# Down weights in four parts, eight rows turned in the first attention, the whole fold in the experts, and a reordered second attention

## What is computed

```python
h = tok(x, W, b)                                   # 256 x 512, patches of 128 samples
h = h + attn0(layernorm(h), Wq, Wk, Wv, Wp)        # 16 heads, ternary weights, int8-like rounding
h = h + moe(layernorm(h), router, gate, up, down)  # 16 experts of width 192, top 2 of them
h = h + attn1(layernorm(h), Wq, Wk, Wv, Wo)        # 16 heads, 4 key heads, causal
h = h + ffn1(layernorm(h), SU_ug, SU_dp, Wscale_ug, Wscale_dp, W_up, W_gate, W_down)

def ffn1(x, ...):                 # n = 512, inner width 2048
    x = fwht(x * SU_ug) / 64      # Walsh-Hadamard transform of width 512
    x_up   = x @ W_up.T   * (Wscale_ug[:2048] * 64)
    x_gate = x @ W_gate.T * (Wscale_ug[2048:] * 64)
    x = silu(x_gate) * x_up
    x = fwht(x * SU_dp) / 64      # transform of width 2048
    return x @ W_down.T * (Wscale_dp * 64)
```

## Time and profile before

| | |
|---|---|
| three runs | 284.29, 284.68, 285.15 us; median 284.68 us |
| the profiled execution | 285.33 us device time, span 283.5 us |
| mean granted clock of PE in it | 0.984 of full speed |
| busy in the span | PE 267.1 us (94%), DVE 228.1 (80%), ACT 148.7 (52%), POOL 6.4 (2%) |
| 40.43 MB moved, mean | 143 GB/s |

### The profile page before, as it was taken

How to read it: one execution, slowest core, us unless ns; L and a number is a source line. 1 busy time by engine, 2 the same in 40 slices (tenths; PEclk the granted TensorE clock), 3 DMA queues, 4 the chain that set the end, 5 groups by cost and what they waited for, 6 DMA issues and landing times. The chain is left out here.

```text
span 283.5 us, 3968 instructions
## 1 busy us (share of the span) xinstructions
PE 267.1 (94%) x1492; PEld 220.5 (78%) x1492; DVE 228.1 (80%) x410; ACT 148.7 (52%) x233; POOL 6.4 (2%) x19
## 2 busy tenths in 40 slices
PE   8789489999999999999999999999999999999993
PEld 3445355858899998989999887775589999999872
DVE  1979998797999978797798876798898895778783
ACT  2898760145563565555565514444457562663530
POOL 0200000000000000000000000000000000000000
PEclk9999959999999999999999999999999999999998
DMA  6960499944244807173530087193000000000003
GB/s 233 424 243 1 116 408 391 410 194 132 91 163 173 333 17 318 45 290 115 218 114 0 0 296 298 28 407 161 0 0 2 0 2 0 0 2 0 0 5 74
DMA packets 6565, 40.43 MB, mean 143 GB/s; under 512 B 1169, under 2 KB 1425, under 8 KB 5266
## 3 DMA queue, kind: packets, MB, share of 16 engines
q1 hardware_dynamic: 6546, 40.18, 36.9%
HBM read 39.13 MB, written 0.52 MB: 140 GB/s over the span
## 5 line engine op out<-in xcount | busy, mean ns | idle before, releaser
L1089 PE MATMUL bank<-s_xf_hi,s_f_hi 128*128 128x256 f32 x128 | 31.4, 284 | 0.0
L1089 PE MATMUL bank<-s_xf_hi,s_f_lo 128*128 128x256 f32 x128 | 31.1, 281 | 0.0
L530 ACT ACTIVATE s_silu<-bank 128x192 f32<-128x192 f32 x32 | 10.5, 331 | 36.6 <-PE bank L868 32.6
L868 PE MATMUL bank<-s_w_hi,s_xt_hi 128*128 128x384 f32 (+1 forms) x128 | 29.2, 350 | 0.0
L868 PE MATMUL bank<-s_w_lo,s_xt_hi 128*128 128x384 f32 (+1 forms) x128 | 27.9, 339 | 0.3 <-DVE s_w_lo L1416 0.3
L868 PE MATMUL bank<-s_w_hi,s_xt_lo 128*128 128x384 f32 (+1 forms) x128 | 27.8, 338 | 0.3 <-DVE s_xt_lo L1179 0.3
L1089 PEld LDWEIGHTS bank<-s_xf_hi,s_f_hi 128*128 128x128 f32 x128 | 24.1, 188 | 1.0 <-issue 0.5
L1089 PEld LDWEIGHTS bank<-s_xf_hi,s_f_lo 128*128 128x128 f32 x128 | 24.1, 188 | 0.4
L1642 DVE TENSOR_TENSOR s_f_lo<-s_ffn_raw,s_f_hi 128x1024 fp32r<-128x1024 f32 x16 | 19.6, 1224 | 5.3 <-ACT s_f_hi L610 5.2
L868 PEld LDWEIGHTS bank<-s_w_lo,s_xt_hi 128*128 128x128 f32 x128 | 22.7, 188 | 0.7 <-DVE s_w_lo L1416 0.7
L868 PEld LDWEIGHTS bank<-s_w_hi,s_xt_lo 128*128 128x128 f32 x128 | 22.8, 188 | 0.5 <-DVE s_xt_lo L1179 0.5
(11 more groups left out here) (241 smaller groups left out, 570.7 us busy)
## 6 DMA issues: line engine op xcount, KB each, us to landing
s_moe_raw<-moe_gu SPq DMA_DIRECT2D x16, 768.0 KB, 6.6
s_ffn_raw<-ffn_w SPq DMA_DIRECT2D x4, 2048.0 KB, 10.0
s_moe_raw<-moe_dn SPq DMA_DIRECT2D x8, 768.0 KB, 4.4
s_big_raw<-att_w SPq DMA_DIRECT2D x4, 1024.0 KB, 8.2
s_big_raw<-down_w SPq DMA_DIRECT2D x1, 4096.0 KB, 18.4
s_l_raw<-l_w SPq DMA_DIRECT2D x1, 2560.0 KB, 25.0
out<-s_h SPq DMA_DIRECT2D x4, 128.0 KB, 2.3
s_tok_w<-tok_w SPq DMA_DIRECT2D x1, 256.0 KB, 2.7
```

The costliest lines, as they stand in the source:

```text
L530: act.activation(B["silu"][i % 2][:], unit_bank(i)[:, 0:F], ACT.Silu).then_inc(silu_done, 1)
L868: ins = pe.matmul(unit_bank(i)[:, 0:n], xt(k, t)[part % 2], w[:, k, 0:n], start=(first and k == 0), stop=(last and k == KC - 1))
L1089: pe.matmul(tb(j, n)[:, 0:TOK], M[w][j][:, k, n * P:(n + 1) * P], M["xf_hi"][:, k, :], start=(w == "w_hi" and k == 0), stop=False)
```

## The change

It has four parts, all in the order of the written-out lists.

1. `down_w` comes in four transfers of 1 MB (rows 0 to 3, 4 to 7, 8 to 11, 12 to 15), each with its own semaphore. The first three are issued between the transfers of `k_swapped` and `v_swapped`, after `side_done` of 6; the fourth stands where the whole one stood.
2. Eight rows are turned in the first attention instead of four: three behind the product of line 822, ahead of the ternary copy; one for each tile in the place of seven filling products; three where three stood before. The one behind the transposes of the experts' input goes. The copies back on ACT move with them: three ahead of the casts of `tern_p`.
3. All 18 operations of the fold stand in the experts (`fold_step(0)` to `fold_step(17)`), three per pair, one of them ahead of `hidden(4 * p)`. `last_fold` goes.
4. In the second attention five turns are spread differently and four go: the turn inside `values(1)`, the turn behind `values(0)` (the identity product with `h` takes its place, so PE adds the residual of tile 0 and ACT copies the sum to `h`), one of three ahead of `values(1)` and the one ahead of the feed-forward. `exp(2)` stands ahead of `kv_out(1)`. DVE's `centred` for tile 0 stands ahead of the two `low_half`.

```diff
@@ names and tables
-        ld_l1, ld_down = sem("ld_l1"), sem("ld_down")
+        ld_l1 = sem("ld_l1")
+        ld_down = [sem(f"ld_down{g}") for g in range(4)]
-        TURNS = (0, 4, 8, 12, 10, 14, 11, 15, 1, 5, 9, 13, 2, 6, 3, 7)
-        TURN_BANK = (7, 3, 7, 3, 5, 1, 5, 1, 5, 1, 2, 5, 0, 4, 0, 4)
-        TURNS_FIRST = 4
+        TURNS = (0, 1, 4, 5, 8, 9, 12, 13, 10, 14, 11, 15, 2, 6, 3, 7)
+        TURN_BANK = (3, 7, 5, 3, 7, 3, 7, 3, 5, 1, 5, 1, 5, 0, 4, 0)
+        TURNS_FIRST = 8
@@ SP
+                if n == 0:
+                    sp.wait_ge(side_done, 6)
+                    for g in range(3):
+                        down_part(g)
...
             sp.wait_ge(side_done, 8)
-            sp.dma_start(big_raw[:], down_w).then_inc(ld_down, 16)
+            down_part(3)
@@ ACT
             exp(0, A["sc"][:, 2], A["sc"][:, 3])
+            for i in range(3):
+                turned_back(i)
             for k in range(KC):
                 act.wait_ge(tern_done, k + 1)
...
             xt_high(0)
+            turned_back(3)
             xt_high(1)
+            turned_back(4)
...
-            for i in range(3):
+            for i in range(5, TURNS_FIRST):
                 turned_back(i)
             xt_high(2)
-            turned_back(3)
...
+            exp(2, L["sc"][:, 2, 0, 0:2], L["sc"][:, 3, 0, 0:2])
             kv_out(1)
-            exp(2, L["sc"][:, 2, 0, 0:2], L["sc"][:, 3, 0, 0:2])
...
             f_high(1)
+            act.wait_ge(proj_done, 3)
+            act.copy(h[:, 0, :], tb(0, 3)[:]).then_inc(h_kept, 1)
             exp(3, L["sc"][:, 2, 1, 0:4], L["sc"][:, 3, 1, 0:4])
@@ PE
-                if i == 0:
-                    pe.wait_ge(ld_down, 16)
+                pe.wait_ge(ld_down[TURNS[i] // 4], 16)
...
+            pe.wait_ge(v16_ready, TILES)
+            turn(0)
+            turn(1)
+            pe.wait_ge(half_ready, 4)
+            turn(2)
             pe.wait_ge(q16_ready, TILES)
...
             for t in range(TILES):
+                pe.wait_ge(turned, t + 1)
                 for c in range(2):
...
                 transposes(t, A["xn"], t)
-                keep_warm(bank[3], FILL)
+                turn(3 + t)
...
                 for s in range(keys):
-                    if s == 2:
-                        turn(11)
                     pe.wait_ge(val_ready, 2 * t + s + 1)
...
             values(0)
-            turn(7)
+            pe.matmul(tb(0, 3)[:], ident, h[:, 0, :], start=True, stop=False)
...
-            for i in (8, 9, 10):
-                turn(i)
-            pe.wait_ge(turned, 11)
+            turn(11)
+            turn(12)
             values(1)
...
-            turn(15)
@@ DVE
             for p in range(2, PAIRS - 1):
                 main_low(2 * p + 1)
                 rest_low(2 * p + 1)
+                fold_step(3 * p - 4)
                 hidden(4 * p)
...
-                fold_piece(p - 1)
+                fold_step(3 * p - 3)
+                fold_step(3 * p - 2)
...
-            fold_piece(PAIRS - 2)
+            fold_step(17)
...
-            dve.wait_ge(proj_done, 3)
-            o.mark(dve.tensor_tensor(h[:, 0, :], tb(0, 3)[:], h[:, 0, :], ALU.add), 0)
+            dve.wait_ge(h_kept, 1)
             moments(0)
+            dve.wait_ge(xnt_done, 9)
+            dve.wait_ge(su_ready, 1)
+            centred(0, h[:, 0, :])
             low_half(8, bank[6], 0)
             low_half(9, bank[2], 1)
-            dve.wait_ge(xnt_done, 9)
-            dve.wait_ge(su_ready, 1)
-            across_chunks(0, h[:, 0, :])
+            across_chunks(0)
...
-            last_fold(0)
             f_low(1)
...
-            last_fold(1)
```

More of the change, by code:

```diff
@@ L361, in _, with down_part @@
         def _(sp):
+            def down_part(g):
+                at = slice(4 * g * C, 4 * (g + 1) * C)
+                sp.dma_start(big_raw[:, at], down_w[:, at]).then_inc(ld_down[g], 16)
             sp.dma_start(bias_row[:], tok_b).then_inc(ld_bias, 16)
@@ L848, in _ @@
                 if t == 0:
-                    keep_warm(bank[3], 3)
-            for i in range(3):
+                    keep_warm(bank[2], 3)
+            for i in range(5, TURNS_FIRST):
                 turn(i)
             transposes(2, B["xn"], 0)
-            turn(3)
             pe.wait_ge(ld_small, 48)
@@ L963, in _ @@
             transposes(4, L["xn"], 0)
-            turn(4)
+            turn(8)
             dn(PAIRS - 1, 1, 1, 3)
@@ L1021, in output_high @@
                 for k in half:
-                    pe.matmul(tb(t, 3)[:], xt(k, t)[0], L["o_hi"][:, k, :], start=(t == 0 and k == 0), stop=False)
+                    pe.matmul(tb(t, 3)[:], xt(k, t)[0], L["o_hi"][:, k, :], start=False, stop=False)
                     pe.matmul(tb(t, 3)[:], xt(k, t)[0], L["o_lo"][:, k, :], start=False, stop=False)
-            turn(5)
-            turn(6)
+            turn(9)
+            turn(10)
             values(0)
-            turn(7)
+            pe.matmul(tb(0, 3)[:], ident, h[:, 0, :], start=True, stop=False)
             pe.wait_ge(o1_ready, 2)
@@ L1060, in lane_transform @@
                 return last
-            pe.wait_ge(turned, 11)
+            pe.wait_ge(turned, 12)
             scaled_transposes(0, range(KC), bank[1])
-            for i in range(12, 15):
+            for i in range(13, 16):
                 turn(i)
-            pe.wait_ge(turned, 12)
+            pe.wait_ge(turned, 13)
+            pe.wait_ge(h_kept, 1)
             scaled_transposes(1, (0, 1), bank[5])
@@ L1153, in normalised, with centred, across_chunks @@
                                          ALU.subtract, ALU.mult)
[L1155 removed]
+            def centred(t, src):
+                o.settle(t)
+                o.mark(dve.scalar_tensor_tensor(M["xn"][:, t, :], src, mv[:, t, 0:1], su_row[:], ALU.subtract, ALU.mult), t)
+            def across_chunks(t):
                 xn, y = M["xn"], M["y"]
                 half = C // 2
[L1159 to L1160 removed]
                 o.settle(t)
@@ L1517, in fold_of, with fold_step @@
                 return (down_raw[:, 2 * (g // 4) + 4 * i:2 * (g // 4) + 4 * i + 2, :] for i in range(4))
-            def fold_even(g):
+            def fold_step(n):
+                g, step = 4 * (n // 9), n % 9
                 s0, s1, s2, s3 = fold_of(g)
-                if g == 0:
-                    dve.wait_ge(ld_down, 16)
+                if n == 0:
+                    for part in ld_down:
+                        dve.wait_ge(part, 16)
                     dve.wait_ge(turned, TURNS_FIRST)
-                o.settle()
-                o.mark(dve.tensor_tensor(fold, s0, s2, ALU.add))
-                o.mark(dve.tensor_tensor(s2, s0, s2, ALU.subtract))
@@ L1566, in fold_piece @@
-            def fold_piece(g):
-                (fold_even, fold_odd, fold_sums, fold_rest)[g % 4](g)
+                to, a, b, op = ((fold, s0, s2, ALU.add), (s2, s0, s2, ALU.subtract),
+                                (s0, s1, s3, ALU.add), (s3, s1, s3, ALU.subtract),
+                                (s1, fold, s0, ALU.subtract), (s0, fold, s0, ALU.add),
+                                (fold, s2, s3, ALU.add), (s3, s2, s3, ALU.subtract), (s2, fold, None, None))[step]
+                if step % 2 == 0:
+                    o.settle()
```

64 lines of the change are left out of this document (18 added, 46 removed).

## The result

| | before | changed |
|---|---|---|
| median, first comparison | 284.91 us (4 runs) | 282.10 us (281.72 to 282.93, 4 runs) |
| ratio, 95% interval | | 0.9878 [0.9832, 0.9923] |
| the profiled execution | 285.33 us, span 283.5 | 282.39 us, span 280.6 |
| mean granted clock of PE in it | 0.984 | 0.996 |

Two later comparisons gave ratios of 0.9900 [0.9858, 0.9942] and 0.9873 [0.9842, 0.9904]. In the comparisons of the experiments the kernel before has a median of 285.0 us (64 runs); the changed one has 282.0 over its three (16 runs). The change is worth some 3 us. The prediction was 281.1, its own range 280.5 to 281.8, and the range with rivals 280.0 to 282.9: the time lies in the wide range and just outside the narrow one, nearer to rival A's 282.4 than to 281.1. That the range held is owed in part to the room left in it for the rivals.

The account below looks back on a forecast made before the run. PE was taken to bound experts and feed-forward, chains of small pieces the attentions; 1.3 + 1.8 + 0.5 = 3.6 us off 285.33 gives 281.7, less 0.65 for the median 281.1, range 280.5 to 281.8 (8 in 10: 280.0 to 282.9).

Parts of the forecast that it names:

- rival A: First attention: the clock falls all the same or the turns come late, so 1.3 us are not won: 282.4; chance 0.17.
- the clock that stays: First attention: with turns in PE's gap the longest pause is under 1 us and the clock stays at 2.4 GHz.
- the split of the first attention: First attention, at 51.37: sums of t = 1 end earlier, so the split loses most of its 0.36 us wait.
- the turn ahead of the feed-forward: Start of the feed-forward: without this turn PE starts when ACT has the first half of `xf_hi`, 0.3 us earlier.
- the first term: First attention: turns in PE's gap keep the clock up, so fillings and sums come earlier: 1.3 us, bounds 0 and 1.6.
- Second term: Second attention, `values(1)`: one turn fewer ahead, no copy wait, none inside; last four sums start 1.86 us earlier, 1.8 carried.
- The move of 0.8 us into DVE's next wait: Second attention: earlier `exp(2)` shrinks DVE's wait by some 0.8 us, which moves into its wait for `values(0)`'s split: 0.
- Third term: Start of the feed-forward: dropping the turn (0.3 us) and `last_fold(0)` (0.15 us and a little more) gains 0.5 us.
- The 0.15 for `last_fold(0)`: Start of the feed-forward: `last_fold(0)` delays `xf_lo`, for which PE waits 0.15 us; a little more in the next chunk.
- The fold: Experts: three more DVE operations, 3.1 to 3.7 us, with 16 us to spare; costed at 0.
- Rival C: First attention: `v_swapped` comes late and DVE waits; slower, 286.5 us at 200 GB/s; chance 0.06.
- Rival D: More is won than counted, because small waits on the shortened ways close too: 279.9 to 280.5 us; chance 0.10.

Follow-up runs that it names:

- experiment 4: The kernel before with only the fold changed, all 18 operations in the experts and no `last_fold`: 284.52 us, ratio 0.9986.
- experiment 2: The kernel before with filling products added in PE's gap ahead of the ternary copy: 17 gave ratio 0.9983; 31, closing the gap within 0.57 us, 284.32 us, 0.9973.
- experiment 7: The changed kernel with the `l1_w` transfer (2.6 MB) moved ahead of `v_swapped` on the same queue: 288.43 us, ratio 1.0105.
- experiment 6: The changed kernel with turn 10 moved from `values(0)` to ahead of `values(1)`: 280.97, then 281.02 us; that plus copy wait and turn inside `values(1)` put back: 283.81 us.
- experiment 5: The changed kernel with two unused turn-shaped products added, one ahead of the second attention's `values(1)` and one inside it: 282.66 us, ratio 0.9926.
- experiment 3: The changed kernel with turns 0 to 2 moved from ahead of the ternary copy to behind it, replacing the 18 filling products: 283.68 us, ratio 0.9950.

## Why the prediction was right or wrong

*The mechanisms* in the first profile stand for the most part where the prediction put them: turns in the gap, no wait at the reduction, full experts of unchanged length, no turn in `values(1)`, an earlier `xf_lo`. Three did not: the clock that stays, the split of the first attention, and the turn ahead of the feed-forward (below). *The sum against the profile* was 3.6 us and is nearly 3.6 by like stretches (1.38, 1.83, 0.35), 2.9 in the pair of profiles, whose starts differ by chance.

*The step that was off,* though the time lies in the range, is the one from the profile to the median: "That execution lies 0.65 us over the median of 284.68, so I predict 281.1 for the median." I took 1.3 us for ending the long fall of the clock, and then took off again the 0.65 by which this execution was slow. By the second profile of before, the long fall is itself 1.08 us of such an execution. Of 64 timed executions of the kernel before, 21 have a mean clock of 0.993 or 0.994 and a median of 284.2 us; 43 have 0.982 to 0.988 and 285.4. The profile I worked from (0.984) belongs to the second kind. The mean clock tells the kinds apart only roughly. It takes in what is granted behind PE's last product, in that profile 0.50 from 281.4 us on; and experiment 4's profile has 0.988 without a long fall, from an early fall at 14.3 us and a short one in the gap. That the gap is behind most of the 43 is likely by experiment 2: with the gap closed two of twelve lie at 0.990 or under, beside 14 of 19 of the kernel before. With the 3.6 taken from its own 285.33, and nothing off, the forecast is 281.7, and the changed kernel's executions lie at 281.6 to 282.9 but for one (284.24), median 282.0. That measured medians lie 2.8 to 3.6 us apart, and not 3.6 each time, is the same: the first term is 0.3 us where the clock comes back early and 1.4 where it doesn't.

*First term.* Right against the profile (1.38 for 1.3), about 0.8 for a median (the closed gap's 0.8). Of the 1.38, 1.05 lies ahead of the first reduction and 0.28 between the two; the second one, before and after:

```profile
50.31 0.69 DVE L1370 TENSOR_REDUCE s_am<-bank 128x16 f32<-128x512 f32 x1 [0.19 <-PE bank L837]
```

```profile
49.66 0.68 DVE L1385 TENSOR_REDUCE s_am<-bank 128x16 f32<-128x512 f32 x1
```

The 0.36 us at the split, which I wanted to win too, is still 0.34 (50.68). The transfers came at the late end of my estimate: the longest pause was 1.06 to 1.45 us, not under 1. The reason "the clock stays at 2.4 GHz" held in half the cases only: of eight profiles with the three turns in the gap, four show no fall there, and four show 0.50 from 34 or 35 us to 37 or 38. In those the turns take 4.4 to 4.5 us, but the clock is back before the fillings, and the stretch is 20.02 to 20.24 us. So *rival A's* mechanism came true in part and without its price: the four with no fall have 20.01 or 20.02 us, but for experiment 7's, which waits for its transfer. Full silence, which I took from the trace of before for what the fall needs, is not needed by these rows. The section of the Trainium skill named there (TensorE: Matmul & The Clock Gate, "Loop structure matters more than you think") shows a product behind a long wait for a transfer, 8 us in its example. Four of the eight profiles agree with it at much shorter pauses, and four don't.

*Second term.* 1.8 predicted, 1.82 and 1.83 measured. It is the wait for the copy back and the turn inside (1.81 by experiment 6); the third turn ahead of `values(1)` was worth nothing (experiment 5). The move of 0.8 us into DVE's next wait was right too (0.32 to 1.16), and experiment 6 got it back.

*Third term.* 0.5 predicted, 0.35 to 0.39 measured, all of it the fold's. The 0.3 for the turn ahead of the feed-forward is wrong: PE then waits 0.54 us for ACT's `xf_hi`, the next thing late. The 0.15 for `last_fold(0)` was too small, since its effect goes on into the second and third chunk (experiment 4: 1.41 us behind, then 1.20 and 1.03).

*Costed at nothing.* The fold: no more than 0.04 us over the experts, with 2.55 us more on DVE where I expected 3.1 to 3.7. `v_swapped`: nobody waited; it is issued at 32.58 and 33.09, 7.6 us from issue to landing, so it is there at about 40.7 and needed at 42.25, 1.5 us to spare and not 2. *Rival C's* mechanism is shown by experiment 7; its price there was 1.9 us more than the wait. *Rival D* came with an edit of its own, not with this change.

## What to carry to other kernels

Before an offset between a profiled execution and the median is carried over, ask whether the thing the change mends is that offset: take a second profile of the kernel before, and look at the mean clock of its timed runs. Here a product inside a chain of sums put off the rest of the chain by its full length (0.86 us), while one ahead of the chain was free up to the wait for data that it covered; moving one turn into such a wait was worth 0.8 us. When you price a stall in a serial stage, ask for the work at half clock behind it too: 4.67 us of waiting came to 6.6.

## What the runs showed of the hardware

- The same program's clock falls at other moments in other executions. In the kernel before the gap of the earlier trace rows (4.18 and 4.44 us) was followed by 1.2 GHz to 42.5 us in one profile and to 40.3 in the other. Pauses of 1.06 to 1.45 us between products, ahead of the turns, were followed by a fall in four profiles and by none in four.
- Four of twelve further profiles (experiments 2, 3, 4 and 6) show an early fall, where no experiment edits anything: a granted clock of 0.50 for some 3 us, from 14.2 to 14.6 us on in three of them and from 15.7 on in the closed gap's. Their first attentions come 1.1 to 2.1 us later than 40.56. This is a part of the scatter of a single run, and why like stretches of two profiles tell tenths that the times don't. What decides it stays open: no run here varies anything ahead of 28 us. It also stays open how many of the 43 executions of the kernel before are due to this and how many to the long fall.
- A transfer of 2.6 MB put ahead of two small ones on one queue delayed them by 6.2 us (13.9 from issue to landing, 7.7 without). So they didn't pass it. The Trainium skill (DMA: Bandwidth & Descriptors, "Queues, rings and completion order") has each DMA engine take descriptors in ring order, and this delay agrees. That a small transfer "cannot pass" was my conclusion: the same section says that a later transfer can complete ahead of an earlier one, which no run here shows.
